# A graph layer pair on one core: raw gathers for the first four groups, rows of 19 groups held, list work moved, edges dealt in eights

## The chip, the core and the metric

The kernel runs on one core of a Trainium2 chip. The core has TensorE (PE, matrix products, with PEld for its weight loads), VectorE (DVE), ScalarE (ACT), GpSimd (POOL) and SyncE (SP, which here only issues DMAs). They run separate instruction streams and meet at semaphores. The metric is the device time of one execution in microseconds, the median of the runs.

## The reference

There are N = 6250 nodes with 64 features and E = 206250 edges, sorted by destination.

```python
h = jnp.maximum(_layernorm(x, axis=-1), 0.0)
# layer 0: messages from (h[src], edge_attr), summed over dst, then an update
m = jax.nn.relu(jnp.concatenate([h[src], edge_attr_64], -1) @ W1 + b1) @ W2 + b2
agg = jax.ops.segment_sum(m, dst, num_segments=6250)
x = x + jax.nn.relu(jnp.concatenate([h, agg], -1) @ U1 + c1) @ U2 + c2
h = jnp.maximum(_layernorm(x, axis=-1), 0.0)
# layer 1: weighted rows of h, summed over dst
x = x + jax.ops.segment_sum(h[src] * edge_weight[:, None], dst, num_segments=6250)
```

## The kernel before

**Tiling.** Edges go in GROUPS = 202 groups of GE = 1024, each of T = 8 tiles of 128 edges. Nodes go in CHUNKS = 10 chunks of 625.

**Start.** For each chunk DVE and ACT compute the layer norm (`centre`, `square`, `variance`, `root`, `normalise`), PE turns it (`turn_h`) and multiplies it by the node half of W1 (`make_t1`), ACT stages the product and SP stores it in the DRAM table `table1`. So one row of `table1` is what a source node adds to the hidden layer of an edge. Meanwhile POOL clears memory, and from src and dst lists are worked out: the source indices `idx`, the place of a destination in its group `rel`, and for layer 1 `lo` and `key`. They lie with one group to a partition (`src_i`, `dst_i`) and are turned by PE (`turn_half`, twenty half tables, j = 0 to 19) and copied back by `keep`. POOL divides the sources by 125 in six instructions (`hi_g`). At the end DVE splits the edge weights into three bf16 parts.

**Gathers.** POOL then issues eight indirect DMAs for each group (L770), one for each tile, 128 rows of 256 bytes each, into `rows`, a ring of RING = 3 groups. `gather1(g)` waits until DVE has used group g - 3 (`pre_made`). POOL issues all 1616 in order.

**The loop over groups** (step s, all engines, `fast_groups`). DVE adds the gathered rows to the product of edge_attr and the lower half of W1 (`add_product`, L1533), ACT takes the relu (`make_hid`), PE sums it over destinations with a 0/1 matrix (`sum_hid`). In the same step DVE makes two "quads" of 0/1 matrices (`make_quad`, L1561, L1558, L1568), and PE builds from them eight tiles of the weighted adjacency (`build_tile`, L1115) for layer 1, which ACT keeps and SP stores. edge_attr comes by one DMA for each group (`load_ea`), is turned (`turn_ea`) and multiplied (`make_q`). Each time enough groups have passed, one chunk of nodes is updated, and later steps multiply stored adjacency by the updated rows (`direct`, `late_products`). After the loop `fast_end` multiplies what is left.

The order on each engine is written out by hand; the compiled program also holds another branch for other inputs (`slow1`, `slow2` and the rest), which these inputs don't enter.

## Time and profile before

| what | us |
|---|---|
| three runs | 3366.19, 3371.68, 3379.27 |
| median | 3371.68 |
| profiled execution, first to last instruction | 2261.6 |
| median less that span | 1110.1 |
| gathers, first start | 51.23 |
| gathers, last start | 2109.06 |
| last addition of gathered rows | 2116.08 |

The page gives no other time for the profiled execution than its span; 1110.1 us of the median lie outside every row of the trace. A busy share is time in which an engine works. Between two gathers POOL's sequencer takes about 0.3 us that isn't counted as busy.

### The profile page before, as it was taken

What the parts mean: (1) busy time and instruction counts of PE and PEld (TensorE: products, weight loads), DVE (VectorE), ACT (ScalarE), POOL (GpSimd) and SP (SyncE); (2) the same over time, 40 slices, a digit from 0 to 9 for tenths busy, and PEclk for the clock granted to TensorE, in tenths of its full rate; (3) what the DMA queues carried; (4) which work ended last, traced back from release to release, by engine and by line L of the source; (5) the groups of instructions that cost most, each with busy time, mean ns of one, the idle gap of its engine ahead of it and who ended that gap; (6) DMA issues with size and microseconds to landing.
All of it is one profiled execution on the core that took longest, in us unless ns stands there. A gap on an engine that the chain in (4) does not pass through costs nothing.

```text
span 2261.6 us, 54037 instructions
## 1 busy us (share of the span) xinstructions
PE 1807.0 (80%) x19448; PEld 1531.0 (68%) x19448; DVE 1650.8 (73%) x4933; ACT 950.1 (42%) x2278; POOL 1605.8 (71%) x1671
## 2 busy tenths in 40 slices
PE   6766767677776787778768877888988888988899
PEld 6555556556665676667657766776877777878787
DVE  7876767677776777777767777777777777877564
ACT  5344444444344444444444444444444433534211
POOL 7777777777777777777777777777777777777200
PEclk9988888888888898899889999999999999999999
DMA  4455556554864595478548856874986688678798
GB/s 104 131 176 185 179 165 215 185 174 154 261 197 148 174 285 178 133 234 268 159 136 261 244 162 180 242 232 136 280 227 188 165 259 257 174 208 258 223 311 283
DMA packets 559732, 459.71 MB, mean 203 GB/s; under 512 B 287224, under 2 KB 507656, under 8 KB 555878
## 3 DMA queue, kind: packets, MB, share of 16 engines
q1 hardware_dynamic: 501386, 401.52, 56.7%
q0 software_dynamic: 51776, 53.07, 9.6%
q8 instruction: 160, 2.62, 0.5%
q10 hardware_dynamic: 6300, 1.60, 0.3%
q14 instruction: 110, 0.90, 0.1%
HBM read 281.45 MB, written 174.54 MB: 202 GB/s over the span
## 4 chain that ended last, share of the span: by engine, by line
POOL 65%; issue 21%; PE 9%; DMA 4%; DVE 1%; SPq 0%; ACT 0%; DVEq 0%; POOLq 0%
POOL rows L770 65%; DMA late_piece<-adjacency 2%; PE pair L1231 2%; DMA stage<-tail 1%; PE pair L1129 1%; PE pair L1026 1%; PE pair L1146 1%; PE pair L1255 1%; PE pair L1115 1%; PE pair L1245 1%; PE pair L1263 0%; PE pair L1014 0%; PE pair L1237 0%; PE pair L1102 0%; DMA rows<-table,idx 0%
## 5 line engine op out<-in xcount | busy, mean ns | idle before, releaser
L770 POOL DMA_INDIRECT rows<-table,idx x1616 | 1566.5, 969 | 494.5 <-issue 492.3
L887 ACT COPY stage<-pair 128x300 f32<-128x300 f32 x1616 | 621.0, 415 | 680.5 <-PE pair L1115 673.5
L1115 PE MATMUL pair<-bld 128*128 128x300 bf16 x4848 | 779.9, 315 | 5.8 <-DVE bld L1558 5.7
L1558 DVE TENSOR_SCALAR bld<-iota_key,key 128x300 bf16<-128x300 f16 x1616 | 595.6, 369 | 119.1 <-PE pair L1115 118.6
L1115 PEld LDWEIGHTS pair<-bld 128*128 128x128 bf16 x4848 | 555.8, 120 | 158.1 <-issue 7.7
L1087 PE MATMUL pair<-w1b,rings 128*128 128x128 f32 x1616 | 284.8, 331 | 387.9 <-DVE rings L1533 387.6
L1087 PEld LDWEIGHTS pair<-w1b,rings 128*128 128x128 f32 x1616 | 246.6, 233 | 432.2 <-DVE rings L1533 431.1
L1568 DVE TENSOR_TENSOR bld<-bld,part 128x512 bf16<-128x512 bf16 x1212 | 475.1, 392 | 0.0
L1533 DVE TENSOR_TENSOR rings<-rows,pair 128x512 f32<-128x512 f32 x202 | 137.7, 681 | 362.7 <-DMA rows<-table,idx 360.2
L878 ACT ACTIVATE rings<-rings 128x512 f32<-128x512 f32 x202 | 127.9, 633 | 301.4 <-DVE rings L1533 301.0
L1129 PE MATMUL pair<-stage,h 125*64 125x96 f32 x4230 | 228.3, 249 | 0.0
L1146 PE MATMUL pair<-late_piece,h 125*64 125x192 f32 x1856 | 201.4, 327 | 27.1 <-DMA late_piece<-adjacency 26.2
L1129 PEld LDWEIGHTS pair<-stage,h 125*64 125x64 f32 x4230 | 199.1, 137 | 0.3 <-issue 0.2
L1146 PEld LDWEIGHTS pair<-late_piece,h 125*64 125x64 f32 x1856 | 145.9, 137 | 34.6 <-issue 30.2
L1561 DVE TENSOR_TENSOR bld<-iota_lo,lo 128x512 bf16<-128x512 f16 x404 | 163.4, 404 | 0.0
L1551 DVE TENSOR_REDUCE hot_sum<-hot 128x40 f32<-128x320 f32 x202 | 156.5, 775 | 6.3
L1102 PE MATMUL pair<-hot,rings 128*64 128x40 f32 x3232 | 134.4, 232 | 0.0
L1102 PEld LDWEIGHTS pair<-hot,rings 128*64 128x64 f32 x3232 | 110.7, 137 | 34.1 <-issue 34.1
L1080 PE MATMUL pair<-ident,rings 128*128 128x128 f32 x808 | 123.5, 276 | 2.4 <-issue 1.7
L873 ACT COPY rings<-pair 128x512 f32<-128x512 f32 x202 | 118.4, 586 | 15.6 <-PE pair L1080 10.7
L1080 PEld LDWEIGHTS pair<-ident,rings 128*128 128x128 f32 x808 | 100.9, 144 | 7.5 <-issue 2.0
L1151 PE MATMUL pair<-late_piece,h 125*64 125x96 f32 x928 | 98.1, 246 | 0.0
(155 smaller groups left out, 1143.0 us busy)
## 6 DMA issues: line engine op xcount, KB each, us to landing
late_piece<-adjacency SPq DMA_DIRECT2D x232, 480.0 KB
rings<-in_edge_attr_dram SPq DMA_DIRECT2D x202, 256.0 KB
adjacency<-stage SPq DMA_DIRECT2D x28, 1080.0 KB
rows<-table,idx POOLq DMA_INDIRECT x1616
tail<-stage SPq DMA_DIRECT2D x202, 120.0 KB
stage<-tail SPq DMA_DIRECT2D x50, 480.0 KB, 5.6
adjacency<-stage SPq DMA_DIRECT2D x20, 960.0 KB
adjacency<-stage SPq DMA_DIRECT2D x20, 840.0 KB
```

The lines of the kernel that those rows point to most:

```text
L770: pool.indirect_dma_start(out=rows[:, slot, t, :], out_offset=None, in_=table, in_offset=bass.IndirectOffsetOnAxis(ap=idx[:, g, t:t + 1], ...
L887: act.copy(tiles[:, g % STAGE, :, t * WT:(t + 1) * WT], build_bank[i % 3][:, 0:KEYS].rearrange("p (h w) -> p h w", w=WT)).then_inc(tile_ke ...
L1080: last = pe.transpose(bank[:, a * P:(a + 1) * P], ea_ring[:, slot, a * P:(a + 1) * P], ident[:, :])
L1087: last = pe.matmul(bank[:, a * P:(a + 1) * P], eaT[:, slot, a, :], w1b2[:, :], start=True, stop=True)
L1102: pe.matmul(half_of(sum_bank, t)[:, 0:W], hid[:, slot, t, 0:D], hot[:, slot, t, :], start=(t < 2), stop=(t >= T - 2))
L1115: last = pe.matmul(build_bank[i % 3][:, 0:KEYS], hot_w[q % 2][k][:, :, u], hot_key[q % 2][:, u, :], start=(k == 0), stop=(k == PARTS - 1))
L1129: last = pe.matmul(half_of(u_bank, h), h2[:, h * D:(h + 1) * D], tiles[0:NP, slot:slot + 2, h, :], start=(h < 2), stop=(h >= many - 2))
L1146: pe.matmul(half_of(mid_bank, h)[:, at:at + QCOLS], h2[:, (c * BLK + h) * D:(c * BLK + h + 1) * D], held[:, :, h, :], start=(h < 2), stop= ...
L1551: dve.tensor_reduce(hot_sum[:, g % TWO, :], hot[:, g % TWO, :, :].rearrange("p t w -> p w t"), AX_X, ALU.add).then_inc(hot_summed, 1)
L1558: return dve.tensor_scalar(hot_key[q % 2][:, u, :], iota_key[:, :], key[:, g, t + u:t + u + 1], None, ALU.is_equal)
L1561: dve.tensor_tensor(hot_eq[q % 2], iota_lo[:, :, :], over(lo[:, g, t:t + 4], P), ALU.is_equal).then_inc(eq_made, 1)
L1568: dve.tensor_tensor(hot_w[q % 2][k], hot_eq[q % 2], over(part[k][:, g, t:t + 4], P), ALU.mult)
```

## The change

- Edges of a group are dealt in runs of eight: partition p holds edges 8p to 8p+7. So `load_ea` reads 2048 contiguous bytes for each partition, where it read eight pieces of 256, and `idx` and `rel` are turned with a stride of eight elements. `lo`, `key` and the weights keep the old order.
- ACT loads the source indices of groups 0 to 3 straight from DRAM. POOL gathers these RAW = 4 groups from the input `x` itself, before the table exists. For them DVE and ACT compute the layer norm for each edge, PE turns the rows and multiplies them by the node half of W1 into the same bank as edge_attr's product, with the bias.
- The rows of groups 0 to 18 go to memory that is idle then (`rows_of`): `late_piece`, `h2`, and the sums' part of `nodes` beyond its first two chunks. For these groups POOL waits only until group g - 3 has landed; from group 22 on it waits for `pre_made` as before. ACT clears the held part of `nodes` at steps 20 to 24.
- List work leaves POOL: the cast of the sources and the two rows of constants go to ACT, the six `hi_g` instructions and eight clears to DVE. ACT takes eight `keep` copies from DVE. The weight load w1a goes from POOL's queue to ACT's.

```diff
+RAW = 4
+IN_H2 = 6
+EARLY = 19
+BOTH = 6
...
+        ROWS = T * D
+        HELD = 2 * CN
+        HELD_END = HELD + (EARLY - RAW - IN_H2) * ROWS
+        assert RAW * ROWS <= LATE * QUAD * CW + 2 * QCOLS and IN_H2 * ROWS <= NB * D and ROWS <= 2 * BC
+        assert HELD_END <= N + W - WB and EARLY > RAW + IN_H2 >= BOTH > RAW and BOTH % RING == 0
+        def flat_rows(g):
+            if g < RAW:
+                return late_all[:, g * ROWS:(g + 1) * ROWS]
+            if g < RAW + IN_H2:
+                return h2_all[:, (g - RAW) * ROWS:(g - RAW + 1) * ROWS]
+            at = N + HELD + (g - RAW - IN_H2) * ROWS
+            return nodes[:, at:at + ROWS]
+        def rows_of(g):
+            if g < EARLY:
+                return flat_rows(g).rearrange("p (t f) -> p t f", f=D)
+            return rows[:, g % RING, :, :]
...
-                rows_of = edge_attr[ds(edge_row(g), GE), :].rearrange("(t p) f -> p t f", p=P)
-                sp.dma_start(ea_ring[:, slot, :].rearrange("p (t f) -> p t f", f=D),
-                             rows_of).then_inc(ea_loaded[slot], 16)
+                rows_of = edge_attr[ds(edge_row(g), GE), :].rearrange("(p t) f -> p (t f)", t=T)
+                sp.dma_start(ea_ring[:, slot, :], rows_of).then_inc(ea_loaded[slot], 16)
...
+                if n == 0:
+                    sp.wait_ge(pre_made, RAW)
...
-            pool.memset(bad[:, :], 0.0).then_inc(consts_set, 1)
-            pool.memset(t_stage[:, :, :], 1.0).then_inc(consts_set, 1)
-            pool.dma_start(w1a[0:D, :], w1[0:D, :]).then_inc(w1_loaded, 16)
-            pool.dma_start(w1a[D:D + 1, :], b1.rearrange("(o f) -> o f", o=1)).then_inc(w1_loaded, 16)
-            pool.wait_ge(consts_set, 6)
-            for c in range(CHUNKS):
-                pool.memset(nodes[D:DEG + 1, c * CN:(c + 1) * CN], 0.0).then_inc(pool_step, 1)
-            pool.wait_ge(pool_step, 3 + CHUNKS)
-            for c in range(CHUNKS):
-                pool.memset(hT[D:D + 1, c * CN:(c + 1) * CN], 1.0).then_inc(ones_set, 1)
-            pool.wait_ge(ones_set, CHUNKS)
-            pool.wait_ge(src_loaded, 80)
-            for h in range(2):
-                n = HALF[h]
-                pool.tensor_copy(src_f[0:n, h, :], src_i[0:n, h, :]).then_inc(src_made, 1)
-            for t in (t_base, t_max, t_min):
...
-            for h in range(2):
-                n = HALF[h]
-                pool.wait_ge(src_made, h + 1)
-                pool.tensor_scalar(hi_g[0:n, h, :], src_f[0:n, h, :], (NP - 1) / 2.0, 1.0 / NP, ALU.subtract,
-                                   ALU.mult).then_inc(hi_made, 1)
...
+            def landed(g):
+                wait_count(pool, gathered[g % RING], (g // RING + 1) * 16 * T)
+            def fast_gather(g):
+                if g >= EARLY + RING:
+                    pool.wait_ge(pre_made, g - RING + 1)
+                elif g >= RING:
+                    landed(g - RING)
+                gather(x if g < RAW else table1, g, rows_of(g))
...
-            pool.wait_ge(consts_set, 14)
-            pool.wait_ge(iotas_set, 2)
-            pool.wait_ge(ones_set, CHUNKS)
+                gather(table2, g, rows[:, g % RING, :, :])
+            pool.wait_ge(idx_loaded, 32)
+            for g in range(RAW):
+                fast_gather(g)
             pool.wait_ge(kept_act, 4)
             for s in range(2):
                 pool.wait_ge(t1_stored[s], 16 * CHUNKS // 2)
-            for g in range(GROUPS):
-                gather1(g)
-            pool.wait_ge(pre_made, GROUPS)
+            for g in range(RAW, BOTH):
+                fast_gather(g)
             pool.wait_ge(fast_made, 2)
             fast = pool.value_load(fast_i[0:1, 0:1], min_val=0, max_val=1)
             with pool.If(fast > 0):
-                pool.nop()
+                for g in range(BOTH, GROUPS):
+                    fast_gather(g)
+                pool.wait_ge(pre_made, GROUPS)
...
+            act.dma_start(idx[:, 0, :], src[E - GE:E].rearrange("(p t) -> p t", t=T)).then_inc(idx_loaded, 16)
+            act.dma_start(idx[:, 1:RAW, :], src[0:(RAW - 1) * GE].rearrange("(g p t) -> p g t", p=P, t=T)
+                          ).then_inc(idx_loaded, 16)
+            act.dma_start(w1a[0:D, :], w1[0:D, :]).then_inc(w1_loaded, 16)
...
+            def sources_as_f32():
+                act.wait_ge(src_loaded, 80)
+                for h in range(2):
+                    n = HALF[h]
+                    act.copy(src_f[0:n, h, :], src_i[0:n, h, :]).then_inc(src_made, 1)
+            def fill_rows(c, slot):
+                act.activation(nodes[D:DEG + 1, c * CN:(c + 1) * CN],
+                               ones[D:DEG + 1, 0:1].to_broadcast([DEG + 1 - D, CN]), ACT.Copy,
+                               scale=fill[D:DEG + 1, 0:1]).then_inc(ones_set, 1)
...
-            unrolled(CHUNKS, ((1, root(1)), (0, square(1)), (2, stage_hT), (3, stage_t1), (3, clear_first)), 10,
-                     keep_sources)
+                    keep(j, idx, RAW if j < 2 else 0)
+            def clear(first, last, cleared):
+                act.activation(sums1[:, first:last], ones[:, 0:1].to_broadcast([P, last - first]), ACT.Copy,
+                               scale=0.0).then_inc(cleared, 1)
+            held_pieces = [HELD + (HELD_END - HELD) * i // 5 for i in range(6)]
+            def clear_held(i):
+                clear(held_pieces[i], held_pieces[i + 1], sums_cleared)
+            unrolled(CHUNKS, ((1, root(1)), (0, square(1)), (0, fill_rows), (2, stage_hT), (3, stage_t1)),
+                     {8: sources_as_f32, 10: keep_sources})
+            for first, last in ((0, CN), (CN, HELD), (HELD_END, N + W)):
+                clear(first, last, sums_cleared)
...
+            for j in range(12, 16):
+                keep(j, key)
+            for j in range(16, 20):
+                keep(j, rel)
...
+            def square_raw(g):
+                act.wait_ge(raw_dve, after_raw(RAW_DVE, "cent", g))
+                act.activation(sq_all[:, 0:ROWS], flat_rows(g), ACT.Square).then_inc(raw_act, 1)
+            def root_raw(g):
+                act.wait_ge(raw_dve, after_raw(RAW_DVE, "var", g))
+                act.activation(e_std[:, :], e_var[:, :], ACT.Sqrt, bias=eps[:, :], scale=1.0 / D).then_inc(raw_act, 1)
+            def keep_raw(g):
+                act.wait_ge(raw_turned, g + 1)
+                wait_count(act, q_made, g)
+                act.copy(e_turned_kept.rearrange("p a e -> p (a e)"), mid_bank).then_inc(raw_act, 1)
...
+                        if s == EARLY + 1:
+                            act.wait_ge(pre_made, EARLY)
+                        if EARLY < s <= EARLY + 5:
+                            clear_held(s - EARLY - 1)
...
+                by_row = of[0:n, h, :].rearrange("g (p t) -> g t p", t=T)
                 for t in range(4 * q, 4 * q + 4):
-                    last = pe.transpose(pair[3][:, j % 2, (t % 4) * P:(t % 4) * P + n],
-                                        of[0:n, h, t * P:(t + 1) * P], ident[0:n, 0:n])
+                    edges = by_row[:, t, :] if of is src_f or of is rel_g else of[0:n, h, t * P:(t + 1) * P]
+                    last = pe.transpose(pair[3][:, j % 2, (t % 4) * P:(t % 4) * P + n], edges, ident[0:n, 0:n])
...
+            def make_raw_q(g, slot, bank):
+                wait_step(pe, eaT_kept, g)
+                pe.wait_ge(raw_act, after_raw(RAW_ACT, "kept", g))
+                for a in range(T // 2):
+                    to = bank[:, a * P:(a + 1) * P]
+                    pe.matmul(to, eaT[:, slot, a, :], w1b2[:, :], start=True, stop=False)
+                    pe.matmul(to, e_turned_kept[:, a, :], w1a2[:, :], start=False, stop=False)
+                    for i in range(2):
+                        last = pe.matmul(to[:, i * D:(i + 1) * D], ones[D:D + 1, :], w1a[D:D + 1, :], start=False,
+                                         stop=(i == 1))
...
+                        if s + 1 < RAW:
+                            turn_raw(s + 1)
+                            pe.wait_ge(pre_made, s + 1)
+                            make_raw_q(s + 1, (s + 1) % TWO, q_bank)
...
+            dve.memset(fill[D:DEG, :], 1.0).then_inc(blank_set, 1)
+            dve.memset(fill[DEG:DEG + 1, :], 0.0).then_inc(blank_set, 1)
+            dve.memset(t_all[0:D + 1, :, :], 1.0).then_inc(blank_set, 1)
+            dve.memset(bad[:, :], 0.0).then_inc(blank_set, 1)
+            for t in (t_base, t_max, t_min):
+                dve.memset(t[:, :, :], 0.0).then_inc(blank_set, 1)
+            dve.memset(base[:, :], 0.0).then_inc(blank_set, 1)
+            dve.memset(t_cols[:, :, :], FAR).then_inc(blank_set, 1)
...
+                dve.wait_ge(src_made, h + 1)
+                dve.tensor_scalar(hi_g[0:n, h, :], src_f[0:n, h, :], (NP - 1) / 2.0, 1.0 / NP, ALU.subtract,
+                                  ALU.mult).then_inc(hi_made, 1)
...
+            def add_fast(g):
+                slot = g % TWO
+                if g >= RAW:
+                    gathered_wait(dve, g, g % RING, 0)
+                dve.wait_ge(q_made, g + 1)
+                wait_count(dve, hid_made, g - TWO + 1)
+                of = q_bank.rearrange("p (t f) -> p t f", f=D)
+                if g < RAW:
+                    dve.tensor_copy(pre[:, slot, :, :], of).then_inc(pre_made, 1)
+                else:
+                    dve.tensor_tensor(pre[:, slot, :, :], rows_of(g), of, ALU.add).then_inc(pre_made, 1)
+            def centre_raw(g):
+                of = rows_of(g)
+                gathered_wait(dve, g, g % RING, 0)
+                dve.tensor_reduce(e_sum[:, :], of, AX_X, ALU.add).then_inc(raw_dve, 1)
+                dve.wait_ge(raw_dve, after_raw(RAW_DVE, "summed", g))
+                dve.tensor_scalar(e_mean[:, :], e_sum[:, :], 1.0 / D, None, ALU.mult).then_inc(raw_dve, 1)
+                dve.wait_ge(raw_dve, after_raw(RAW_DVE, "mean", g))
+                dve.tensor_tensor(of, of, spread(e_mean[:, :], D), ALU.subtract).then_inc(raw_dve, 1)
+            def variance_raw(g):
+                dve.wait_ge(raw_act, after_raw(RAW_ACT, "sq", g))
+                dve.tensor_reduce(e_var[:, :], sq_all[:, 0:ROWS].rearrange("p (t f) -> p t f", f=D), AX_X,
+                                  ALU.add).then_inc(raw_dve, 1)
+            def normalise_raw(g):
+                of = rows_of(g)
+                dve.wait_ge(raw_act, after_raw(RAW_ACT, "std", g))
+                dve.reciprocal(e_rstd[:, :], e_std[:, :]).then_inc(raw_dve, 1)
+                dve.wait_ge(raw_dve, after_raw(RAW_DVE, "rstd", g))
+                dve.scalar_tensor_tensor(out=of, in0=of, scalar=0.0, in1=spread(e_rstd[:, :], D), op0=ALU.max,
+                                         op1=ALU.mult).then_inc(raw_dve, 1)
...
             def fast_groups():
+                centre_raw(0)
+                make_quad(0)
+                variance_raw(0)
+                normalise_raw(0)
+                make_quad(1)
                 for s in range(GROUPS + 6):
                     if s < GROUPS:
-                        add_product(s, s, q_bank)
+                        add_fast(s)
                         make_hot(s)
-                    if s == 0:
-                        make_quad(0)
-                        make_quad(1)
+                    if s + 1 < RAW:
+                        centre_raw(s + 1)
+                    if s == EARLY + 8:
+                        dve.wait_ge(sums_cleared, 8)
...
+                        if q % 2 == 0 and s + 1 < RAW:
+                            variance_raw(s + 1)
+                            normalise_raw(s + 1)
```

POOL, from the constants of the start to the gathers. Before (`iota_key` and `iota_lo` are constants, L757 to L766 the divisions):

```order
L750 IOTA iota_key 128x300
L752 IOTA iota_lo 128x512
L757 TENSOR_SCALAR stage<-stage 102x1024
L757 TENSOR_SCALAR stage<-stage 100x1024
L762 TENSOR_SCALAR stage<-stage 102x1024
L762 TENSOR_SCALAR stage<-stage 100x1024
L766 TENSOR_SCALAR stage<-stage 102x1024
L766 TENSOR_SCALAR stage<-stage 100x1024
L770 DMA rows<-table,idx 128x64 x1616
```

The same place of the changed kernel:

```order
L785 IOTA iota_key 128x300
L787 IOTA iota_lo 128x512
L792 DMA late_piece<-in_x_dram,idx 128x64 x32
L792 DMA h<-table,idx 128x64 x16
L828 TENSOR_LOAD fast_i
L828 ISA x2
L829 COMPARE_AND_BRANCH
L792 DMA h<-table,idx 128x64 x32
L792 DMA nodes<-table,idx 128x64 x72
L792 DMA rows<-table,idx 128x64 x1464
```

The divisions are gone, 32 gathers read `x`, and POOL's branch now stands after the sixth group.

PE, from the branch on to the end of the first step. Before (`rings` holds edge_attr and its turned copy, `bld` the quads, `hot` the 0/1 matrix of destinations):

```order
L1080 MATMUL pair<-ident,rings 128x128 x8
L1087 MATMUL pair<-w1b,rings 128x128 x4
L1115 MATMUL pair<-bld 128x300 x9
L1087 MATMUL pair<-w1b,rings 128x128 x4
L1115 MATMUL pair<-bld 128x300 x15
L1080 MATMUL pair<-ident,rings 128x128 x4
L1102 MATMUL pair<-hot,rings 64x40 x8
L1105 MATMUL pair<-hot_sum,ones 64x40
```

The changed kernel, from the last of the four products of group 0 to the first of group 1:

```order
L1198 MATMUL pair<-w1b,rings 128x128
L1199 MATMUL pair<-w1a,t_stage 128x128
L1201 MATMUL pair<-w1a,ones 128x64 x2
L1229 MATMUL pair<-bld 128x300 x24
L1175 MATMUL pair<-ident,rings 128x128 x4
L1216 MATMUL pair<-hot,rings 64x40 x8
L1219 MATMUL pair<-hot_sum,ones 64x40
L1189 MATMUL pair<-ident,late_piece 128x128 x4
L1198 MATMUL pair<-w1b,rings 128x128
L1199 MATMUL pair<-w1a,t_stage 128x128
L1201 MATMUL pair<-w1a,ones 128x64 x2
```

In the first three steps the product for the next group has moved from behind the third tile to the end of the step, and behind four transposes of the raw rows.

## Rows read from the trace of the kernel before

**Rows 1.** The page: the span, and the longest chain's shares by engine.

```profile
span 2261.6 us, 54037 instructions
...
POOL 65%; issue 21%; PE 9%; DMA 4%; DVE 1%; SPq 0%; ACT 0%; DVEq 0%; POOLq 0%
```

**Rows 2.** The page's groups: busy us, mean ns of one, then idle before and its releaser.

```profile
L770 POOL DMA_INDIRECT rows<-table,idx x1616 | 1566.5, 969 | 494.5 <-issue 492.3
...
L1087 PE MATMUL pair<-w1b,rings 128*128 128x128 f32 x1616 | 284.8, 331 | 387.9 <-DVE rings L1533 387.6
...
L1533 DVE TENSOR_TENSOR rings<-rows,pair 128x512 f32<-128x512 f32 x202 | 137.7, 681 | 362.7 <-DMA rows<-table,idx 360.2
...
L873 ACT COPY rings<-pair 128x512 f32<-128x512 f32 x202 | 118.4, 586 | 15.6 <-PE pair L1080 10.7
```

**Rows 3.** Timeline of POOL (start, duration): gathers number 1, 15, 33, 177 and 1616.

```profile
51.23 1.47 POOL L770 DMA_INDIRECT rows<-table,idx  x1 [2.27 <-DMA table<-h]
...
72.26 2.61 POOL L770 DMA_INDIRECT rows<-table,idx  x1 [0.30 <-issue]
...
98.39 0.94 POOL L770 DMA_INDIRECT rows<-table,idx  x1 [0.30 <-issue]
...
282.05 0.94 POOL L770 DMA_INDIRECT rows<-table,idx  x1 [0.30 <-issue]
...
2109.06 0.95 POOL L770 DMA_INDIRECT rows<-table,idx  x1 [0.30 <-issue]
```

**Rows 4.** Timeline of DVE: the additions of groups 0, 3, 4, 5, 6 and 201.

```profile
78.92 0.69 DVE L1533 TENSOR_TENSOR rings<-rows,pair 128x512 f32<-128x512 f32 x1 [1.26 <-issue]
...
105.90 0.69 DVE L1533 TENSOR_TENSOR rings<-rows,pair 128x512 f32<-128x512 f32 x1
112.91 0.69 DVE L1533 TENSOR_TENSOR rings<-rows,pair 128x512 f32<-128x512 f32 x1
123.83 0.69 DVE L1533 TENSOR_TENSOR rings<-rows,pair 128x512 f32<-128x512 f32 x1 [3.74 <-DMA rows<-table,idx]
132.00 0.69 DVE L1533 TENSOR_TENSOR rings<-rows,pair 128x512 f32<-128x512 f32 x1
...
2116.08 0.68 DVE L1533 TENSOR_TENSOR rings<-rows,pair 128x512 f32<-128x512 f32 x1
```

**Rows 5.** Timeline of POOL: the longest constant of the start.

```profile
28.39 1.19 POOL L752 IOTA iota_lo<- 128x512 f16 x1
```

**Rows 6.** DMA issues: a small load during the loads of x (KB, us to landing).

```profile
w1a<-in_L_gnn_W_dram POOLq DMA_DIRECT2D x1, 16.0 KB, 2.4
```

**Rows 7.** Timeline of PE: first transpose, source transposes, last products for the table.

```profile
11.55 1.22 PE L1014 MATMUL pair<-ident,hot 125*64 125x125 f32 x5 [11.55 <-DVE hot L1369]
...
35.23 1.57 PE L998 MATMUL pair<-ident,stage 102*128 102x102 f32 x8
...
42.51 4.30 PE L1026 MATMUL pair<-w1a,nodes 65*125 65x64 f32 x20
```

**Rows 8.** Timeline of DVE: the second mean, beside POOL's clears.

```profile
7.76 2.54 DVE L1351 TENSOR_SCALAR mean<-row_sum 125x5 f32<-125x5 f32 x1
```

**Rows 9.** Timeline of ACT in a chunk's turn: its idle time before the copy, and what ended it.

```profile
32.44 0.43 ACT L831 COPY h<-pair 125x320 f32<-125x320 f32 x1 [0.88 <-PE pair L1026]
```

**Rows 10.** Timeline of DVE: one pass over half a list, two steps of the weight split.

```profile
64.32 0.62 DVE L1480 TENSOR_SCALAR stage<-stage,base 100x1024 f32<-100x1024 int32 x1
...
71.87 1.84 DVE L1501 TENSOR_TENSOR bld<-bld,part 128x1616 f32<-128x1616 f32 x1
73.75 1.00 DVE L1503 CAST part<-bld 128x1616 bf16<-128x1616 f32 x1
```

**Rows 11.** Two steps: busy us (x count) of PE, PEld, DVE, ACT, POOL; granted clock, DMA share, GB/s.

```profile
98.69:105.90 7.21, 5.50 (x54) 4.65 (x54) 7.13 (x21) 4.34 (x10) 5.59 (x6) 1.00 0.68 220
123.83:132.00 8.17, 7.43 (x54) 5.82 (x54) 7.03 (x22) 3.83 (x9) 6.08 (x7) 0.70 0.22 47
```

**Rows 12.** SP's DMA queue: the first five loads of edge_attr (start, us until issued).

```profile
63.60 26.30 SPq L584 DMA_DIRECT2D rings<-in_edge_attr_dram  x5
```

180 lines of the change are left out of this document (106 added, 74 removed).

## The prediction

> **What bounds the kernel now.** I read the page first: the longest chain lies 65% on POOL and 21% on "issue" [rows 1]. The groups say what that is: 1616 gathers of 969 ns, 1566.5 us busy, and 494.5 us between them, of which 492.3 is POOL's own issuing [rows 2]. The remaining 2.3 us is the wait of the first gather for the table. So POOL never waited for a free slot of the ring: once started, it gathers without a pause, 1.27 us each. From number 33 to number 1616 it takes 2109.06 - 98.39 = 2010.7 us for 1583 intervals, 1.270 us, or 10.16 us a group [rows 3].
>
> The other side of the ring waits: DVE's additions wait 360.2 us in all for gathered rows [rows 2]. The timeline of the additions shows what the loop can do without that wait: 105.90 to 112.91 is 7.0 us a step, then 10.9 with a wait of 3.74 [rows 4]. In such a step DVE is busy 7.13 of 7.21 us and PE 5.50 [rows 11]: DVE would be the next bound, at 7.0 to 7.2.
>
> The end hangs on the same pace. The last gather starts at 2109.06, its addition is at 2116.08, and 145.5 us follow to 2261.6, which the change leaves as they are. So the sum is: when the gathers start, whether they ever pause, and whether they stay at 1.27 us.
>
> **The change, part by part.**
>
> *Start of the gathers.* Before, gather 1 starts at 51.23, waiting for the table. Now the first 32 need only the constants and the indices of four groups. POOL's constants that stay take about 5 us; the longest, iota_lo, 1.19 us [rows 5]. The indices come by two DMAs of ACT, while x is being loaded; a load of 16 KB in that time landed in 2.4 us [rows 6]. Theirs is 512 pieces of 32 bytes. Bounds: 5 us (the constants alone) and 12 us (were they queued behind most loads of x). I take 6, nearest to the small load. 32 gathers at 1.27 to 1.35 end at 47 to 49 us.
>
> *The table.* The fifth group still needs it. PE's first transpose was at 11.55, late because DVE's mean of 5 values took 2.54 us beside POOL's clears [rows 7, 8]. With the clears gone most of that goes, and PE starts 2 to 3 us sooner. DVE's new clears of its own lie before x arrives. Against that: ACT now casts the sources in its eighth turn, about 2.2 us for 2 x 1024 elements at the rate of its copy of 512 in 0.586 [rows 2], against a slack of 0.9 us in a chunk [rows 9], so 1 to 1.5 us come back on PE. The transposes of the sources, 1.57 us for each half list, two of them on this path [rows 7], now read with a stride of 32 bytes: between 0 and 3 us more, I take 1. PE's last products for the table ended at 46.8; now about 46, and gather 33 starts at 50.5 (48 to 54). The raw gathers are done by then, so the table decides, and a later index load is hidden up to 3 us. Before, gather 33 started at 98.39 [rows 3].
>
> By the Trainium skill, page "SBUF — State Buffer", section "SBUF: two separate sides", whichever of a DVE instruction in a two-port mode and a GpSimd instruction starts first keeps the shared port for its whole duration. That speaks against gathering during the layer norm: each mean could wait up to one gather. At 0.94 us a mean and 0.9 us slack in each chunk that would cost the table 1 to 2 us, which lies within its bounds above.
>
> *List work beside the gathers.* Before, gathers 1 to 32 took 98.39 - 51.23 = 47.2 us instead of 32 x 1.25 = 40: list work on DVE stretches them, as 72.26, 2.61 us long beside a subtraction of 1.84 and a cast of 1.00 [rows 3, 10]. That is 7.2 us. The same list work now falls on gathers 33 and later, so the 7.2 us remain. The six divisions come to DVE: 6 x 0.62 to 0.75 = 4 us [rows 10], stretching the gathers by 0 to 4; I take 2.8. Together 10 us.
>
> *Sum for POOL.* Gather 177, the first of group 22: before 282.05 [rows 3], 183.7 after number 33. Now 50.5 + 10 + 183.7 = 244.2. That is 37.9 us sooner, **if the rows of groups 4 to 21 have room.** They have, by the held memory; from gather 177 on POOL waits for DVE's addition of group 19.
>
> *Does the loop catch up by then?* DVE's first addition was at 78.92 [rows 4]. Its list work grows by the divisions (+4) and loses eight copies to ACT (about -5, now under the split); the layer norm ends 1 us sooner. The loop starts at about 76. Group 0 then needs, in series: centring (three operations, 1.6), a quad (2.4), variance, root and scaling (2.0), PE's transposes, ACT's copy (0.59) and the products (double of 284.8 / 202 = 1.4, plus bias: 3) [rows 2]. The first addition is at 86. In steps 0 to 2 DVE has six more operations, four of them over 512 elements at 0.68: 3.3 us on top of 7.1, and PE's transposes, ACT's copy and products (4.2) are covered by only one quad (2.4): 12 us a step. Additions: group 3 at 122, group 4 at 129, group 19 at 129 + 15 x 7.1 = 235.5, done at 236.2. That is 8 us before POOL asks (244.2). So no pause. After that POOL's 10.16 us against 7.1 keeps it ahead, and the loop reaches the gathers near group 25.
>
> *At nothing.* Clearing the held memory, five ACT instructions of 1.1 us (922 elements each) at steps 20 to 24: ACT is busy 4.3 of 7.2 us in a step [rows 11], and DVE asks only at step 27; uncovered they would cost 5 us. Loads of edge_attr in pieces of 2048 bytes: SP needed 26.3 us for the first five [rows 12], and nobody waited for one on the path; their cover is the gathers. SP's wait before the first late load is over by step 3. Adding from the held memory costs what adding from the ring does.
>
> **Sum.** Span 2261.6 - 37.9 = 2223.7. The page gives no other time of the profiled execution; the median of the runs is 1110.1 us longer than its span, in no row, and I leave that as it is: 3371.7 - 37.9 = **3334 us**.
>
> **Rivals.**
>
> *Late catch-up, 3350.* The margin is 8 us over 20 steps. In gather-paced steps the granted clock was 0.70 (partly 1.2 GHz, for 1.00 is 2.4), and the step took 8.17 us with PE busy 7.43 instead of 5.50 [rows 4, 11]. If raw steps take 15 and the other fifteen 7.9: 86 + 45 + 8 + 118.5 + 0.7 = 258, POOL pauses 14 us, gain 24, 3348. With a start of the loop 4 us later 3352. For it: chains of four engines in raw steps. Against it: four steps without a wait for rows at full clock and 7.0 to 7.2 us.
>
> *PE stays at 1.2 GHz, slower, 3400.* PE's 5.50 us at 2.4 GHz would be 11 at 1.2, more than DVE's 7.1. Raw steps of 16 and fifteen steps of 11 put the addition of group 19 at 86 + 48 + 11 + 165 + 0.7 = 311, after 282.05: 29 us slower than before. It decides from a step of (282 - 129) / 15 = 10.2 us on. Against it: before, the same step ran at clock 1.00 where nothing waited, and the clock fell only once PE had waited for rows. The Trainium skill, page "TensorE: Matmul & The Clock Gate", section "HAM oscillation — how this bites in real kernels", has idle gaps between bursts put the clock down each time; by that rule raw steps with gaps could start this rival, but a catching-up loop has none, as these rows show.
>
> *Late table, 3341.* Strided transposes at +3 us, means waiting for gathers, a later cast: gather 33 at 57 instead of 50.5, gain 31. It is within my range.
>
> *The part outside the span grows.* The compiled program now has 1616 more gathers in the branch that isn't taken. No row shows what the 1110 us are. If it grew with anything of that, the gain could vanish; 40 us would need 4% of it.
>
> *More gain, 3322.* In the last steps PE waited for late loads of adjacency behind other DMAs; eight times fewer pieces of edge_attr could speed them. POOL's pace bounds that to some us. Gathers beside a calmer DVE could bring 5 more.
>
> **How the numbers follow.** My forecast (gain 28 to 45) has 0.63, with the late table in it; late catch-up (gain 5 to 28) 0.16; more gain 0.07; PE at 1.2 GHz 0.04; outside part or another pause that I don't see 0.10, half of it slower. The likeliest is 3334. The range reaches from 3318 (gain 54) to 3360 (gain 12), which leaves out the slower cases and the tails. Within 0.5%, which is 17 us and about what a measurement can tell from no change, are gains under 17: half of late catch-up and half of the unseen, 0.15. Faster: 0.77. Slower: 0.08.
>
> **What would show it.** POOL's first gather near 6 us, gather 33 near 50 with the wait for the table before it; mean gather 0.96 to 0.98 us; no wait of POOL for an addition from gather 177 on (if there is one, its length is what is lost); first addition near 86, three steps of 12, then 7.1 at clock 1.00; the last gather near 2071 and the end 152 us behind. I am wrong if gathers in the layer norm take over 1.5 us, if POOL waits at group 22, or if span and median don't move together.

## The result, and the profile after

| | us | runs |
|---|---|---|
| before, timed beside it | 3375.47 | 3366.19 to 3391.32, 4 runs |
| after | 3458.7 | 3442.68 to 3475.01, 4 runs |
| after / before | 1.0222 | 95% interval 1.0184 to 1.026 |

The change makes the kernel 2.2% slower; 3334 us had been forecast. The profiled execution of after took 3465.35 us and its span is 3463.5. So nothing lies outside the span. The page of after, first and fourth parts:

```profile
span 3463.5 us, 54291 instructions
...
PE 47%; another core or an unknown queue 28%; issue 14%; DVE 6%; ACT 3%; DMA 1%; DVEq 0%; SPq 0%; ACTq 0%
```

Beside [rows 1], POOL has gone from the chain that ended last, and 28% of it is a releaser that the profile can't name. The groups (as in [rows 2]; busy us, mean ns of one, then idle before and its releaser):

```profile
L792 POOL DMA_INDIRECT rows<-table,idx x1464 | 1401.2, 957 | 1651.8 <-DVE rings L1676 1243.9
L955 ACT COPY stage<-pair 128x300 f32<-128x300 f32 x1616 | 624.2, 415 | 1530.3 <-remote 840.5
```

A gather costs what it did (957 ns), but POOL now waits 1243.9 us for additions: it no longer bounds the kernel alone. ACT's copies of the tiles wait 840.5 us for something called "remote": the semaphore's update came when no instruction and no DMA of the trace had just ended that could have made it. POOL's timeline at the places of [rows 3], gathers 1, 33, 177 and 1616:

```profile
4.91 1.10 POOL L792 DMA_INDIRECT late_piece<-in_x_dram,idx  x1 [0.43 <-DMA idx<-in_src_dram]
...
75.44 5.95 POOL L792 DMA_INDIRECT h<-table,idx  x1 [29.09 <-DMA table<-h]
...
431.18 0.95 POOL L792 DMA_INDIRECT rows<-table,idx  x1 [164.74 <-DVE rings L1676]
...
3288.55 0.94 POOL L792 DMA_INDIRECT rows<-table,idx  x1 [0.30 <-issue]
```

The first gather starts where it was forecast, near 6. The table is 25 us late, and gather 177 waits 164.74 us. DVE's timeline of the additions of groups 0 to 5 (L1674 is a raw group's; answers to [rows 4]):

```profile
122.65 0.69 DVE L1674 COPY rings<-pair 128x512 f32<-128x512 f32 x1 [15.02 <-remote]
...
286.58 0.69 DVE L1674 COPY rings<-pair 128x512 f32<-128x512 f32 x1 [97.50 <-remote]
...
304.18 0.69 DVE L1674 COPY rings<-pair 128x512 f32<-128x512 f32 x1 [7.44 <-PE pair L1201]
322.28 0.69 DVE L1674 COPY rings<-pair 128x512 f32<-128x512 f32 x1 [7.90 <-PE pair L1201]
331.25 0.69 DVE L1676 TENSOR_TENSOR rings<-h,pair 128x512 f32<-128x512 f32 x1
337.85 0.69 DVE L1676 TENSOR_TENSOR rings<-h,pair 128x512 f32<-128x512 f32 x1
```

One step takes 164 us. In it POOL gathers without a pause until 266, and nearly nothing else moves. Once POOL stands still, and the raw groups are through, a step takes 6.6 us. Both stretches by engine, then PE's granted clock, DMA share and GB/s (columns as in [rows 11]):

```profile
122.00:266.00 144.00, 13.32 (x61) 8.88 (x61) 9.58 (x25) 5.60 (x13) 108.96 (x116) 1.00 0.17 37
332.00:430.00 98.00, 82.46 (x810) 69.58 (x810) 96.90 (x314) 63.60 (x150) 0.00 (x0) 1.00 0.62 226
```

In the first, PE, DVE and ACT are busy for under a tenth of 144 us, and the DMA engines are idle for the most part. The clock of 1.00 in that row is no reading: this trace has no record of the clock before 293.5 us, and a stretch without one is printed as 1.00. PE's products there take as long as others do at 0.50 (shown below), so PE ran at 1.2 GHz. On ACT's timeline the first tile copies of this stretch are:

```profile
128.93 0.41 ACT L955 COPY stage<-pair 128x300 f32<-128x300 f32 x1 [21.44 <-remote]
136.62 0.41 ACT L955 COPY stage<-pair 128x300 f32<-128x300 f32 x1 [7.29 <-remote]
145.02 0.41 ACT L955 COPY stage<-pair 128x300 f32<-128x300 f32 x1 [7.99 <-issue]
```

PE's tiles (three products each) beside them:

```profile
116.38 2.44 PE L1229 MATMUL pair<-bld 128*128 128x300 bf16 x9
129.39 0.94 PE L1229 MATMUL pair<-bld 128*128 128x300 bf16 x3 [10.57 <-issue]
137.18 0.92 PE L1229 MATMUL pair<-bld 128*128 128x300 bf16 x3 [6.84 <-issue]
```

One copy comes about every 8 us, where eight come in a step of 6.6 beside a quiet POOL. The three tiles that ACT copies at 128.93, 136.62 and 145.02 had been built by 118.82. The other way nothing is late: PE goes on 0.05 and 0.15 us after a copy of ACT has ended. So what comes late is what PE hands over. The trace of before has nothing like it, though it gathers all the time: this is what the experiments had to explain.

### The profile page after: what moved, and what is told of

It reads as the page before. It is cut to its first block, busy times and chain, and to the rows that moved or that the text cites. A ratio compares the mean times of both kernels' runs of the same rounds, so it can differ in the third digit from the quotient of the medians.

```text
span 3463.5 us, 54291 instructions
## 1 busy us (share of the span) xinstructions
PE 2206.0 (64%) x19560; PEld 1685.7 (49%) x19560; DVE 1593.8 (46%) x4964; ACT 951.5 (27%) x2308; POOL 1561.7 (45%) x1635
## 4 chain that ended last, share of the span: by engine, by line
PE 47%; another core or an unknown queue 28%; issue 14%; DVE 6%; ACT 3%; DMA 1%; DVEq 0%; SPq 0%; ACTq 0%
PE pair L1229 21%; PE pair L1243 6%; PE pair L1260 5%; PE pair L1182 4%; PE pair L1175 3%; PE pair L1216 3%; ACT stage L955 2%; DVE bld L1733 1%; DVE bld L1723 1%; PE pair L1350 1%; PE pair L1265 1%; PE pair L1287 1%; DMA stage<-tail 1%; DVE rings L1676 1%
## 5 line engine op out<-in xcount | busy, mean ns | idle before, releaser
L792 POOL DMA_INDIRECT rows<-table,idx x1464 | 1401.2, 957 | 1651.8 <-DVE rings L1676 1243.9
L1229 PE MATMUL pair<-bld 128*128 128x300 bf16 x4848 | 938.0, 343 | 773.5 <-issue 415.0
L955 ACT COPY stage<-pair 128x300 f32<-128x300 f32 x1616 | 624.2, 415 | 1530.3 <-remote 840.5
L1723 DVE TENSOR_SCALAR bld<-iota_key,key 128x300 bf16<-128x300 f16 x1616 | 509.6, 315 | 876.8 <-PE pair L1229 504.7
L1243 PE MATMUL pair<-stage,h 125*64 125x96 f32 x4230 | 314.6, 276 | 114.1 <-issue 112.9
L1243 PEld LDWEIGHTS pair<-stage,h 125*64 125x64 f32 x4230 | 253.9, 157 | 140.0 <-issue 139.6
L1260 PE MATMUL pair<-late_piece,h 125*64 125x192 f32 x1856 | 252.5, 367 | 37.5 <-issue 35.6
L1711 DVE TENSOR_TENSOR nodes<-nodes,pair 128x40 f32 x202 | 38.6, 191 | 349.1 <-remote 329.3
L1216 PE MATMUL pair<-hot,rings 128*64 128x40 f32 x3232 | 163.0, 257 | 5.4 <-issue 5.4
L1175 PE MATMUL pair<-ident,rings 128*128 128x128 f32 x808 | 159.0, 332 | 7.2 <-ACT rings L941 5.6
L1175 PEld LDWEIGHTS pair<-ident,rings 128*128 128x128 f32 x808 | 133.4, 180 | 20.8 <-ACT rings L941 6.0
```

Of the source, the lines that this page charges most:

```text
L792: pool.indirect_dma_start(out=to[:, t, :], out_offset=None, in_=table, in_offset=bass.IndirectOffsetOnAxis(ap=idx[:, g, t:t + 1], axis=0), ...
L955: act.copy(tiles[:, g % STAGE, :, t * WT:(t + 1) * WT], build_bank[i % 3][:, 0:KEYS].rearrange("p (h w) -> p h w", w=WT)).then_inc(tile_ke ...
L1175: last = pe.transpose(bank[:, a * P:(a + 1) * P], ea_ring[:, slot, a * P:(a + 1) * P], ident[:, :])
L1216: pe.matmul(half_of(sum_bank, t)[:, 0:W], hid[:, slot, t, 0:D], hot[:, slot, t, :], start=(t < 2), stop=(t >= T - 2))
L1229: last = pe.matmul(build_bank[i % 3][:, 0:KEYS], hot_w[q % 2][k][:, :, u], hot_key[q % 2][:, u, :], start=(k == 0), stop=(k == PARTS - 1))
L1243: last = pe.matmul(half_of(u_bank, h), h2[:, h * D:(h + 1) * D], tiles[0:NP, slot:slot + 2, h, :], start=(h < 2), stop=(h >= many - 2))
```

## The experiments

The kernels ran on six chips. On three of them the kernel before takes about 2267 us, on the other three 3390 to 3437, as in the measurement above (3375); they are called the 2267 chips and the 3400 chips below. One of the 3400 chips was met twice, 53 minutes apart, and was slow both times; each other chip was met once. So whether the pace belongs to the chip or to what surrounded it isn't shown, and the chip of the measurement isn't on record. "Before" with a number is always the kernel before timed beside the experiment, on the same chip, and a ratio is made with it alone.

**Before, once more.** No edit.

> The kernel before, unchanged, once more with its profile. Its recorded profile had a span of 2261.6 us while its runs took 3366 to 3391; the changed kernel's profile had a span of 3463.5 us, 1.9 less than the same run's time, and in it additions came every 7.2 and then 22 us while POOL gathered, and every 6.6 us while POOL waited. Theory A: the runs of the kernel before go the same slow way, and the recorded profile of before caught another pace; then this profile has a span near 3370, no unexplained 1110 us, and steps of about 16 us. Rival B: the kernel before has 1110 us outside its span and gathers without a pause; then the span is near 2261 again, beside a time near 3370.

It took 2268.69 us, 1.0006 of before (2266.78, 9 runs), and its page reads:

```profile
span 2266.6 us, 54037 instructions
...
L770 POOL DMA_INDIRECT rows<-table,idx x1616 | 1566.2, 969 | 494.6 <-issue 492.3
```

These are the rows of the trace ahead of the prediction ([rows 1, 2]), and the span is the time less 2 us. So that trace came from an execution of some 2263 us, and the three times of 3366 to 3379 beside it from other conditions. The 1110.1 us are no part of an execution. The pace was the quick one, so neither theory was met as it stood: A is right that there are two paces, B has the span but not the time.

**After, once more, and its two larger parts one at a time (a 3400 chip).** After unchanged; then without run-ahead:

```diff
-                if g >= EARLY + RING:
+                if g >= BOTH:
                     pool.wait_ge(pre_made, g - RING + 1)
```

then without raw gathers (`RAW = 0`, the first rows read from `table1` after its store, the loop's start as before), with the run-ahead kept:

```diff
-RAW = 4
+RAW = 0
+HOLD = 4
```

and the kernel before with only the edges dealt in eights.

> The changed kernel unchanged, on a chip whose pace for the kernel before is read in the same job. The kernel before took 3371 us in one job and 2267 us in another, with the same instructions, so the pace of a job has to be read first. Theory A (two paces of the surroundings): where the kernel before takes about 2267, the changed one has no pauses of 8 to 90 us, and my sum holds: 2229 us, POOL without a wait at gather 177, a step of 7.1. Where the kernel before takes about 3370, the changed one takes 3440 to 3475 again. Rival B: the changed kernel itself causes the long pauses (POOL running ahead starves the other engines); then it is slower than before on both, by 2% or more.

> The changed kernel, but from group 6 on POOL waits for the addition of group g - 3, as the kernel before does for every group: no run ahead. Catch-up theory (mine): the loop's first addition is near 86 and the next three take 12 us each, so group 6 is gathered only from 122 on instead of from 80; POOL then runs at 10.2 us a group, and gather 49 at 122 against 147 in the kernel before gives a gain of some 15 to 25 us less than with the run ahead: 2245 to 2255 where before is 2267. Rival (the run ahead is what hurts): this one is faster than the changed kernel.

> The changed kernel without raw gathers: groups 0 to 3 are gathered from the table too, into the same held memory, with no layer norm for each edge; the loop starts as in the kernel before. My sum: the gathers start at 49 to 51 as before, so nothing of the 38 us is gained: 2265 where before is 2267. Rival (raw gathers and raw steps cost more than they give, through POOL's presence beside the layer norm and the steps of 12 us): this one is faster than the changed kernel.

> The kernel before with one part of the change alone: edges of a group dealt in runs of eight (edge_attr loaded in pieces of 2048 bytes instead of 256; sources and places of destinations turned with a stride). My sum put this at nothing, within 3 us. Rival: DMA traffic slows the loop, and seven eighths fewer pieces of edge_attr give 1% or more.

| kernel (before: 3435.8 us, 13 runs) | us | ratio | 95% interval | addition 20 at |
|---|---|---|---|---|
| after | 3498.43 | 1.0178 | 1.0123 to 1.0232 | 440.41 |
| without run-ahead | 3475.47 | 1.0105 | 1.0057 to 1.0154 | 410.75 |
| without raw gathers | 3485.63 | 1.0131 | 1.0082 to 1.018 | 424.32 |
| before, dealt in eights | 3423.59 | 0.996 | 0.9929 to 0.9992 | 378.05 |

Each of the two parts loses by itself, less together than their sum (2.4%); the dealing gains 0.4%. Taking one part out makes the changed kernel 23 and 13 us shorter, with runs that overlap (3485 to 3505 for after, 3468 to 3499 and 3475 to 3496), so which of them weighs more isn't told. The step of 164 us is the run-ahead's: without it additions 0 and 1 are at 118.85 and 136.05. The late table is the raw gathers': without them the first gather from it starts at 51.33. In after the loss is made before addition 20: there it is 62 us behind the dealt kernel in the profiles of this chip (440.41 to 378.05), and 60 at the last (3342.37 to 3282.4). The dealt kernel is the nearest to before of which this chip gave a trace (before itself is only timed beside the others). Its groups, then three of its additions in the middle of the loop:

```profile
L769 POOL DMA_INDIRECT rows<-table,idx x1616 | 1551.3, 960 | 1656.5 <-DVE rings L1533 1199.9 <-issue 454.3 <-DMA table<-h 2.3
...
L886 ACT COPY stage<-pair 128x300 f32<-128x300 f32 x1616 | 625.5, 414 | 1618.0 <-remote 917.2
```

```profile
511.44 0.69 DVE L1533 TENSOR_TENSOR rings<-rows,pair 128x512 f32<-128x512 f32 x1
...
518.64 0.69 DVE L1533 TENSOR_TENSOR rings<-rows,pair 128x512 f32<-128x512 f32 x1
...
541.22 0.67 DVE L1533 TENSOR_TENSOR rings<-rows,pair 128x512 f32<-128x512 f32 x1
```

POOL's last gather of the run in between, and ACT's next tile copy:

```profile
531.33 0.94 POOL L769 DMA_INDIRECT rows<-table,idx  x1 [0.31 <-issue]
535.50 1.04 ACT L886 COPY stage<-pair 128x300 f32<-128x300 f32 x3 [18.17 <-remote]
```

So the kernel before, too, is bound otherwise here than its trace tells: POOL waits 1199.9 us, and steps of 7.2 us take turns with steps of 22. POOL issues 16 gathers from 512.40 to 532.27, then waits 9.9 us; the others work on until 517, ACT waits 18.17 us for a tile, and only when POOL has stopped do they go on. From addition 40 to 201 a step takes (3282.4 - 668.7) / 161 = 16.2 us: near POOL's 10.2 **plus** the others' 7, not the longer of the two.

The n-th tile of PE can be held against its n-th copy by ACT through the whole trace: of 1616 copies 289 start more than 1 us after both the tile was done and ACT was free, up to 22.1 us. In the trace ahead of the prediction none does (0.4 at most). The other way, of 190 waits of PE over 1 us before a tile 184 end within 0.2 us of the copy that frees its bank (PE writes its tiles to three banks in turn), and no relu of ACT is more than 0.04 us late behind DVE's addition.

**After on a 2267 chip, and without both parts.** After unchanged; then after with `RAW = 0` and the ring's waits from group 3 on, which leaves the list work moved and the dealing.

> The changed kernel once more, unchanged, to meet the other pace if this job has it. Where the kernel before takes about 2267: theory A, my sum holds, 2229; rival, its early gathers hurt there too, 2290 or more. Where the kernel before takes about 3430: 3490, as in the last job.

> The changed kernel with neither raw gathers nor run ahead: the table for all groups, the ring's wait from group 3 on; what stays of the change is the list work on ACT and DVE and the edges dealt in eights. At the pace of about 3430 for the kernel before: if raw gathers and run ahead are the whole loss, this one equals the kernel before or the one with dealt edges (3424 to 3436, ratio 0.996 to 1.0); rival: moved list work costs something of its own, 1.005 or more.

Before took 2270.18 us (13 runs). After took 2246.13 (ratio 0.9891, 0.9863 to 0.9918), the kernel without both 2273.82 (1.0014, 1.0001 to 1.0026). So on this chip the change does what it was forecast to do, at 24.0 us instead of 37.9, and the run-ahead with the raw gathers brings all of it. A loss by the changed kernel itself, whatever the pace (rival B of the second run), is out. After's POOL at gathers 33 and 177, and DVE's first four additions:

```profile
54.56 2.34 POOL L792 DMA_INDIRECT h<-table,idx  x1 [3.58 <-ACT lo L884]
...
258.03 0.95 POOL L792 DMA_INDIRECT rows<-table,idx  x1 [12.23 <-DVE rings L1676]
```

```profile
90.19 0.69 DVE L1674 COPY rings<-pair 128x512 f32<-128x512 f32 x1 [8.85 <-PE pair L1201]
...
105.75 0.69 DVE L1674 COPY rings<-pair 128x512 f32<-128x512 f32 x1 [5.91 <-PE pair L1201]
...
123.88 0.69 DVE L1674 COPY rings<-pair 128x512 f32<-128x512 f32 x1 [7.77 <-PE pair L1201]
...
140.74 0.69 DVE L1674 COPY rings<-pair 128x512 f32<-128x512 f32 x1 [6.28 <-PE pair L1201]
```

Every raw addition waits for L1201, the bias products. PE's timeline of one of four parts of group 0's product:

```profile
83.50 0.80 PE L1198 MATMUL pair<-w1b,rings 128*128 128x128 f32 x2
84.09 0.64 PE L1199 MATMUL pair<-w1a,t_stage 128*128 128x128 f32 x2
84.66 1.11 PE L1201 MATMUL pair<-w1a,ones 1*128 1x64 f32 x4
```

A part starts every 2.2 us, four make 8.8, and nearly half is bias (each product stands as two records). A part of group 1, in a stretch whose clock is on record at the upper level (95.1 to 101.9 us), takes 1.2:

```profile
99.14 0.46 PE L1198 MATMUL pair<-w1b,rings 128*128 128x128 f32 x2 [0.77 <-ACT t_stage L989]
99.44 0.39 PE L1199 MATMUL pair<-w1a,t_stage 128*128 128x128 f32 x2
99.75 0.65 PE L1201 MATMUL pair<-w1a,ones 1*128 1x64 f32 x4
```

The granted clock of that product, of the second raw step and of the steps from 150 to 257 us (windows of this kernel, columns as in [rows 11]):

```profile
78.00:91.00 13.00, 11.63 (x44) 9.57 (x45) 4.01 (x12) 1.72 (x4) 9.95 (x11) 0.50 0.22 46
105.00:123.00 18.00, 15.09 (x83) 11.55 (x83) 9.76 (x27) 5.19 (x13) 13.73 (x15) 0.69 0.35 108
150.00:257.00 107.00, 84.10 (x810) 70.64 (x810) 104.96 (x317) 64.28 (x151) 73.21 (x75) 0.98 0.68 235
```

The raw steps run at 0.69, a mixture of 1.2 and 2.4 GHz, with PE busy 15.1 of 18 us; the steps after them at 0.98, with DVE busy 105.0 of 107.

**Without the bias products.** It fell on a 3400 chip.

```diff
-                    pe.matmul(to, e_turned_kept[:, a, :], w1a2[:, :], start=False, stop=False)
-                    for i in range(2):
-                        last = pe.matmul(to[:, i * D:(i + 1) * D], ones[D:D + 1, :], w1a[D:D + 1, :], start=False,
-                                         stop=(i == 1))
+                    last = pe.matmul(to, e_turned_kept[:, a, :], w1a2[:, :], start=False, stop=True)
```

> The changed kernel without the eight bias matmuls of each raw group (it leaves out b1 for groups 0 to 3). At the quick pace the first addition came at 90.2 instead of 86, the raw steps took 15.6, 18.1 and 16.9 us instead of 12, and POOL paused 12.2 us at gather 177. Theory A (the bias matmuls, 1.11 us for two pairs at half clock, which my 3 us for the products undersized, are a good part): the first addition at 88 or earlier, raw steps 2 to 4 us shorter each, the pause at gather 177 at 0 to 4 us, the ratio 0.985 to 0.987 (7 to 11 us below the changed kernel's 0.989). Theory B (the hand-overs between DVE, ACT and PE make the steps long, matmuls lie beside them): steps less than 1 us shorter, the pause at 9 to 12, the ratio 0.988 to 0.990. At the slow pace A and B both expect 1.015 to 1.02 and tell nothing.

3443.82 us, ratio 1.0181 (1.0113 to 1.0249; before 3390.18): as after, which both theories had said for this chip. From addition 1 to 4 its trace has 40.6 us instead of 44.7. What it would do to the 12 us pause on a 2267 chip stays untested.

**Neither part, on a 3400 chip.** The edit of above.

> The changed kernel without its two larger parts: no raw gathers and no held rows; only the list work moved off GpSimd and the edges dealt in eights. At the quick pace (the kernel before at about 2270 us) this was 1.0014 of before. What is asked is the same at the slow pace, where the kernel before takes about 3430. Theory A (the slow pace charges for what is done beside gathers, and the two larger parts bring the whole loss of 1.8%; dealing alone gave 0.4%): ratio 0.994 to 0.998, 3416 to 3430 us. Theory B (list work on DVE beside gathers is itself a good part of the loss): ratio 1.005 or more, over 3450. At the quick pace both say 1.000 to 1.003 again, and nothing is told apart.

3382.47 us, ratio 0.9982 (0.9942 to 1.0022; before 3390.18). Theory A, and B is out: moving list work to DVE and ACT costs nothing that can be measured here (on the 2267 chip 3.6 us, together with the dealing); the two parts bring the loss on this chip.

**Plain DMAs in the place of gathers.** One for a whole group, or one for each gather:

```diff
-                    pool.indirect_dma_start(
-                        out=rows[:, slot, t, :], out_offset=None, in_=table,
-                        in_offset=bass.IndirectOffsetOnAxis(ap=idx[:, g, t:t + 1], axis=0),
-                    ).then_inc(gathered[slot], 16)
+                    pool.dma_start(rows[:, slot, t, :], table[t * P:(t + 1) * P, :]).then_inc(gathered[slot], 16)
```

> The kernel before with each group's eight gathers replaced by one plain DMA of POOL's queue that brings 1024 neighbouring rows in 128 pieces of 2048 bytes; so it leaves out the choice of rows by source. POOL is nearly idle. Theory (POOL's gathers hold up the hand-overs between the other engines): steps take 7 to 9 us throughout whatever the pace of the chip, and the time is 1700 to 1950. Rival (the slow pace is of the chip's DMAs or of its clock, not of the gathers): steps stay near 15 us and the time at 3000 or more where the kernel before takes 3430.

> The kernel before with each gather replaced by a plain DMA of POOL's queue for 128 neighbouring rows of 256 bytes: as many instructions of POOL, as many pieces and as many completions as before, no indices; it leaves out the choice of rows by source. If what holds the others up is the building of descriptors or the completions of POOL's DMAs, steps are still long while POOL issues, in proportion to its time (0.6 to 0.75 us each instead of 0.95 + 0.3): 10 to 13 us a step, 2300 to 2900 in all at the slow pace. If it is the indirect form alone, the time is near that of the single plain DMA.

> The kernel before, each gather replaced by a plain DMA of 128 neighbouring rows from POOL's queue, 1616 in all (it leaves out the choice by source). At the quick pace it took 1820. At the slow pace, theory A (the 1616 indirect DMAs, the time in which POOL works out their descriptors, are what holds up the other engines' hand-overs): it stays near 1820, at most 1850, and the slow pace is gone; steps of 7 to 8 us without those of 22. Theory B (the chip is slow in itself, in memory or in semaphores, whoever issues): over 2200 us. Between them, 1850 to 2200, each POOL DMA holds the others up for a share of its time.

On a 2267 chip 1822.2 and 1820.34 us, which shows the pace of the others (some 450 us below before), but not the question. On a 3400 chip the second kernel took 1827.5 beside 3390.18 of before. **The difference between the chips is gone with the indirect DMAs.** The slower chip is not slow in its engines, nor in the DMAs that this kernel keeps. Its POOL group:

```profile
L770 POOL DMA_DIRECT2D rows<-table x1616 | 869.3, 546 | 736.8 <-DVE rings L1530 697.7
```

**Indirect with neighbouring rows, and half of the gathers indirect (a 3400 chip).** First `ap=idn[:, t:t + 1]`, where `idn` holds 0 to 1023 for every group; then every odd tile by the plain DMA of above.

> The kernel before with all 1616 gathers indirect, but their indices are always 0 to 1023, so each reads 128 neighbouring rows (it leaves out the choice by source). At the slow pace (before about 3400), theory A (the indirect DMA as such, its descriptors worked out from indices, holds up the other engines): over 3250 us, steps of 7 and of 22 us. Theory B (rows scattered over the table are what is slow): under 2400. At the quick pace both expect 2240 to 2270, as POOL's 1.27 us a gather bound it there, and only the granted time of a gather can be read.

> The kernel before with every second gather replaced by a plain DMA of 128 neighbouring rows: 808 indirect, 808 plain (it leaves out the choice by source for half of the tiles). POOL needs 4 x (1.27 + 0.57) = 7.4 us a group. At the slow pace, theory A (each indirect DMA holds the others up, so the loss goes by their number): 1827 + half of (3390 - 1827) = 2608 us, 2450 to 2750. Theory B (a loss only once POOL is never idle and its queue is full): under 2050. At the quick pace both expect 1830 to 1900.

3409.96 and 1864.71 us; before 3431.85, one run each. Scattered rows are not the cause: the indirect DMA as such is. But half of them cost next to nothing (1864.71 for 1827.5 with none, on another 3400 chip), where 2608 had been expected from a price for each. Theory A of the half kernel falls. The group shows gathers a little longer than before's 0.97 us:

```profile
L773 POOL DMA_INDIRECT rows<-table,idx x808 | 829.0, 1026 | 358.9 <-issue 219.5 <-DVE rings L1536 134.6 <-DMA table<-h 4.9
```

Two things differ from before: each indirect DMA has a plain one behind it, and POOL has room. The last runs keep all 1616 gathers, so that POOL has less room than before, not more.

**All gathers, with something small between them.**

```diff
+                    if t % 4 == 3:
+                        at = g * 2 + t // 4
+                        pool.dma_start(between[:, at:at + 1], src[0:1].rearrange("(o e) -> o e", o=1)
+                                       ).then_inc(between_set, 16)
```

and the same behind each gather and behind each second one; `between` is a scratch row in DRAM. The clear, behind each gather:

```diff
+                    pool.wait_ge(between_set, g * T + t)
+                    pool.memset(between[:, 0:1], 0).then_inc(between_set, 1)
```

> The kernel before, and behind each of its 1616 gathers a plain DMA of 4 bytes from POOL's queue (0.56 us each). POOL then needs 8 x 1.85 = 14.8 us a group, 2990 us for all, plus 51 at the start and 152 at the end: 3190 if the others are never held up. Theory A (a hold-up needs indirect DMAs close behind each other): 3150 to 3230 at either pace, at the slow one 200 below before. Theory B (each indirect DMA holds the others up, and the half kernel was quick only because it had room): over 3600 at the slow pace.

> The kernel before with a plain DMA of 4 bytes behind every fourth gather. POOL needs 10.16 + 2 x 0.57 = 11.3 us a group, 2283 in all, about 2490 with start and end if the others are never held up. At the slow pace, theory A (a run of more than four indirect DMAs is what holds the others up, any plain DMA ends it): 2450 to 2550, 900 below before. Theory B (it is the pace of 1.25 us, also within four): over 3300. Between them: the hold-up is shortened by it.

> The kernel before with a clear of one element on POOL behind each gather (0.1 us and its issue: 1.35 to 1.5 us a gather), and no DMA more. If the others are never held up: 2400 to 2650. At the slow pace, theory A (any other instruction between two indirect DMAs ends the hold-up): 2400 to 2650. Theory B (only a plain DMA, or the larger distance in time, does): over 3300.

> The kernel before with a plain DMA of 4 bytes behind every second gather. POOL needs 8 x 1.25 + 4 x 0.6 = 12.4 us a group, 2505 in all, 2710 with 51 at the start and 152 at the end. At the slow pace, theory A (hand-overs are held from the start of a run of indirect DMAs to the next plain one, so two cost at most 2.5 us of delay and DVE's work covers it): 2700 to 2800, 0.79 to 0.82 of before. Theory B (within a run the others lose its whole length, whatever its length, and only single gathers let them pass): 3000 to 3250, no better than each fourth. At the quick pace: 2700 to 2720, 1.19 of before.

| behind | chip | us | before | ratio | 95% interval |
|---|---|---|---|---|---|
| each gather, DMA | 3400 | 3211.32 | 3436.74 | 0.9322 | 0.9226 to 0.9419 |
| each fourth, DMA | 3400 | 3205.31 | 3436.74 | 0.9305 | 0.9207 to 0.9403 |
| each gather, clear | 3400 | 3490.05 | 3436.74 | 1.0131 | 1.0026 to 1.0237 |
| each second, DMA | 2267 | 2741.66 | 2267.83 | 1.2081 | 1.2055 to 1.2107 |

1616 useless DMAs of 4 bytes make the kernel 6.8% **faster** on a 3400 chip. The groups of that kernel, then of the one with the clears:

```profile
L772 POOL DMA_INDIRECT rows<-table,idx x1616 | 1654.6, 1024 | 491.9 <-issue 489.7 <-DMA table<-h 2.2
L778 POOL DMA_DIRECT2D between<-in_src_dram x1616 | 897.7, 556 | 0.0
```

```profile
L772 POOL DMA_INDIRECT rows<-table,idx x1616 | 1552.0, 960 | 1529.8 <-DVE rings L1537 1243.0 <-issue 283.5 <-DMA table<-h 2.2
L777 POOL MEMSET between<- 128x1 int32 x1616 | 190.8, 118 | 1.0
```

In the first POOL never waits for an addition any more: it alone sets the pace, 14.9 us a group (additions 40 to 201: 2399 / 161) where 14.8 was worked out, and the others keep up. Held against PE's tiles as above, none of its 1616 copies is over 1 us late (0.9 at most). As POOL is never idle there, theory B of the half kernel (a loss only once POOL is never idle) falls too. In the second the hold-up is as before (290 late copies), so its theory A falls; the clear lies in the 0.30 us between two gathers and doesn't even lengthen them. With a DMA behind each fourth, the hand-overs can be watched. POOL's timeline and ACT's, of the same stretch:

```profile
923.77 0.57 POOL L778 DMA_DIRECT2D between<-in_src_dram  x1
...
929.37 0.57 POOL L778 DMA_DIRECT2D between<-in_src_dram  x1
```

```profile
922.23 0.24 ACT L901 COPY stage<-pair 128x96 f32<-128x96 f32 x1 [6.77 <-remote]
923.71 0.41 ACT L893 COPY stage<-pair 128x300 f32<-128x300 f32 x1 [1.25 <-remote]
...
929.38 0.41 ACT L893 COPY stage<-pair 128x300 f32<-128x300 f32 x1 [3.07 <-remote]
```

Two of these copies start within 0.06 us of a plain DMA. Over 900 to 1500 us ACT has 50 such waits for "remote" of more than 1 us; 31 of them end between 0.35 us before and 1.33 us behind the start of a plain DMA. These stretches are 1.68 us long and there are 83 in 600 us, so 12 would by chance; their bounds were chosen after looking. So what PE hands over is late while POOL issues indirect DMAs 1.25 us apart, and a plain DMA lets some of it through. Behind each fourth it is late more often but by less (413 copies of 1616, up to 11.8 us), POOL waits 736.3 us for additions, and a step takes 15.2 us; the time, 3205, lies between both theories of that run. Behind each second gather, on a 2267 chip, the small DMAs only cost what POOL's 12.6 us a group make of them (2742, just over the 2700 to 2720 expected): there, no hand-over is late that they could free. So no one version was shown to beat both kernels on both kinds of chip: the small DMAs behind each gather win 7% on a 3400 chip, those behind each second lose 21% on a 2267 chip.

## Why the prediction was wrong

**The step that failed** is the last one of the sum: "the median of the runs is 1110.1 us longer than its span, in no row, and I leave that as it is". I named the risk (a part outside the span that grows, and "if span and median don't move together"), but took the 1110 us for a constant beside the execution. They were the same loop at another pace. Every profiled run of these experiments is some 2 us longer than its span, so a median half as long again says that the traced execution isn't one of those timed. The whole argument (POOL bounds all, [rows 1 to 3]) then described only a chip on which 37.9 of 2262 us are at stake. For the other one the trace holds no row: the steps of [rows 4] and 10.16 us a group leave 3372 - 2262 unexplained, and steps in which POOL's 10.16 us and the others' 7 lie behind each other would have been a reading of it, in hindsight: 202 x 7 is 1414, of which 1110 is most. In place of an unchanging 1110 us the runs showed late hand-overs from PE, on which the change itself bears.

**On a 3400 chip** each term turned:

- *Start of the gathers:* 4.91 us for 6, right.
- *Table, gather 33 at 50.5:* 75.44. The raw gathers run during the layer norm, whose chunks pass through four engines; before, POOL had no gathers to issue there. From 5 to 50 us PE is busy 16.5 us and ACT 15.0, where the kernel without raw gathers has 34.5 and 31.4. The rule of the page "SBUF — State Buffer" of the Trainium skill on the shared port, which I had allowed 1 to 2 us, doesn't cover it: PE and ACT wait as well.
- *First addition at 86:* 122.65. The dealt kernel, whose start is that of before, has 85.69.
- *The held rows:* before, the ring of three groups stops POOL at the latest 24 gathers ahead, and in its wait the others catch up. The held memory takes this stop away: POOL gathers from 122 to 266 while the loop makes one step, then stands still for 164.74 us while the loop makes 18 steps, 15 of them of 6.6. Neither hides behind the other. Run-ahead only moves gathers, and gains nothing where time is gather time plus the others' time. Gather 177 came at 431.18, where the dealt kernel has 360.45.
- *Raw steps:* 17.6 and 18.1 us beside a quiet POOL, 11 more than the 6.6 of later steps; the two add 22 us that nothing gives back (the third lies in the 164). Against these losses stand 32 gathers, some 40 us, done before the table.

**On the 2267 chips** the mechanism was right and the size was off, and it was the rival *late catch-up* that came true (gain 24 forecast, 24.0 measured). That its number fits is in part luck: it had raw steps of 15 us and later ones of 7.9, and they were 16.9 and 7.1.

- Gathers stretched by list work, 7.2 + 2.8: gather 177 was ready to start at 245.8 (258.03 less its wait of 12.23), 1.6 us later than my 244.2. The table was 4.1 late and the stretch 2.5 less than my 10.
- The table: gather 33 at 54.56, not 50.5. Its row names `lo` as what it waited for, but POOL waits only for the first four copies of `keep`, and the fourth was done at 37.05. The last store of the table landed at 53.69: it was the table, as forecast, 4 us late. Gather 32 took 4.01 us.
- The mis-sized term: "the products ... plus bias: 3". They took 8.8 us. At the upper clock level the four parts would be 4 x 1.21 = 4.8, of which the bias is 2.4 where I had 0.2; the other 4.0 us are the lower level (0.50), where I had counted with 1.00, as in the raw steps behind it (0.69). So the first addition was at 90.2 instead of 86, and the steps behind it 15.6, 18.1 and 16.9 instead of 12.
- After them came one step of 9.7 and then steps of 7.0 to 7.2, as forecast, but addition 19 came at 257 instead of 235.5, and POOL paused 12.2 us. The forecast said that such a pause is what is lost: 37.9 less 12.2 less 1.6 is 24.1. The profiled execution, the longest of the four (2250.84), has less: from gather 177 on its gathers took 8.8 us more in all than before's, and the last started at 2093.96, 15.1 us sooner than before's. So the fit to 0.1 us is luck too.
- PE's clock was 0.50 at the first raw product and 0.69 in the raw steps, but it rose with the first even steps (0.98): the rival with PE at 1.2 GHz didn't come. The rule of gaps between bursts, from the page "TensorE: Matmul & The Clock Gate" of the Trainium skill, section "HAM oscillation — how this bites in real kernels", can't be read from these rows: PE's gaps are 0.8 to 1.8 us in the raw steps and 0.9 to 1.7 in the even ones, and PE was busy 84% and 79% of them. List work moved at next to no cost (3.6 us with the dealing), and the clears of held memory weren't seen: right.

**Half right, of no use:** that DVE at 7.1 us is the next bound. With plain DMAs in the place of gathers the kernel took 1820 and 1827 us. DVE was busy 105.8 of the 107 us from 103 on (a step of 6.6), but from 800 to 1200 us PE was busy 386 of 400 and DVE 358, and from addition 40 to 201 a step took 8.2.

**A slip in the chances.** By the parts that the text names, "within 0.5%" is 0.08 + 0.05 = 0.13, faster 0.78 and slower 0.09, not 0.15, 0.77 and 0.08.

**Open:** what on a 3400 chip makes PE's hand-overs late. Shown is that it takes indirect DMAs about 1.25 us apart, that neighbouring rows don't help, that a clear between them doesn't, and that a plain DMA does. Whether the plain DMA acts by its kind or by the 0.6 us that it takes was not separated; a clear long enough to take as much would tell. Nor was the kernel with one behind each second gather timed on that chip, where it may be the quickest: POOL's 12.6 us a group would allow some 2740.

## What to carry to other kernels

Hold the span of the trace against the times of the runs before any row is used: here they agree within some 2 us when they belong together, and where they didn't the trace showed another execution than those timed, and the sum made from it didn't hold. More run-ahead for an engine pays only where its work is shown to lie beside the others' work; two steps' lengths that take turns (7 and 22 us) were the sign here that it didn't. Where DMAs of POOL seem to slow engines that wait for none of them, replace them by plain ones in a test: one run then tells what they cost. A clock of 1.00 at the start of a trace is to be held against the length of the products.

## What the runs showed of the hardware

- On three chips of six, while POOL issues indirect DMAs every 1.25 us, what PE hands to ACT or DVE is often late, in one stretch one tile in 8 us, at most by 22.1 us; what ACT and DVE hand over wasn't found late. The kernel before takes 3390 to 3437 us there and 2267 to 2270 on the others; without indirect DMAs 1827.5 and 1820.3. In the trace of the dealt kernel these waits stand as "remote", 917.2 us at the tile copies alone. "issue" alone is no sign: with a small DMA behind each gather no copy is late, though its row has 235.1 us of it.
- A plain DMA from the same queue between any two indirect ones removes it, by its kind or by the time that it takes, even one of 4 bytes (0.56 us): 0.9322 of the time, with 1616 DMAs more. The page "DMA: Bandwidth & Descriptors" of the Trainium skill, section "SWDGE vs HWDGE vs iDMA", has direct and indirect DMAs of GpSimd made by the same software on its cores; these runs show that they are not alike in what they do to others.
- An indirect DMA of 128 rows takes POOL 0.94 to 1.03 us and 0.30 to the next; a plain DMA of as many bytes 0.55, and nearly nothing to the next.
- An f32 product of one row with 64 columns takes about as long as one of 128 rows with 128: 0.52 and 0.57 us at a granted clock of 0.50 (two of the first in 84.66 to 85.70, one of the second in 84.09 to 84.66), 0.30 and 0.31 at the upper level (99.75 to 100.34, 99.44 to 99.75).
- A row of the granted clock can be empty. The trace of after prints 1.00 up to 293.5 us, where its first record stands; until then a part of a raw product takes 2.19 us (109.80 to 111.99), as at 0.50 on the 2267 chip, and not 1.2.
- A single gather among list work and the last of the layer norm took up to 4.01 us on a 2267 chip and 5.95 on a 3400 chip, for 0.94 to 0.97 else.
